# Output phase of an attention kernel: the product with the reciprocals moves ahead of the moments on DVE, and the packing of denominators moves ahead of two other transfers on the sync engine

## The reference

```python
q = q * dh ** (-0.5)
sim1 = jnp.einsum('bhid,bhjd->bhij', q, k_l)
attn1 = jax.nn.softmax(sim1, axis=-1)
out = attn1 @ attn2_inv @ (attn3 @ v)
res = conv_general_dilated(v, conv_w, ...)      # 33 taps along the tokens, one filter a head
out = (out + res).transpose(0, 2, 1, 3).reshape(b, n, h * dh)
out = out @ w_out + b_out
return x + out
...
t = t + _L1_attn_ref(_ln_t(t), ...)             # then t + _L1_ffn_ref(_ln_t(t), ...)
```

## Time and profile before

| | |
|---|---|
| median of 3 runs | 6015.71 us (6015.61 to 6017.85) |
| the profiled execution | 6021.51 us, span 6019.8 us |
| busy in the span | PE 5283.7 us, ACT 3257.7 us, DVE 2981.2 us, POOL 1675.8 us |
| DVE's first and last `o_t` of the output phase | 2643.2 us and 3699.1 us |
| DMA | 755.65 MB in all, a mean of 126 GB/s |

### The profile page before, as it was taken

The page is one execution under the profiler, slowest core; times in us unless marked ns, Lnnn a source line. Parts: engine busy times, 40 slices in busy tenths (PEclk is TensorE's granted clock), DMA queues, the critical chain, the costliest instruction groups (busy, mean ns, idle before and its releaser), DMA issues. The chain is left out here.

```text
span 6019.8 us, 209173 instructions
## 1 busy us (share of the span) xinstructions
PE 5283.7 (88%) x90148; PEld 3236.3 (54%) x90240; DVE 2981.2 (50%) x7660; ACT 3257.7 (54%) x9351; POOL 1675.8 (28%) x2016
## 2 busy tenths in 40 slices
PE   5499999997788887789999997888888888888888
PEld 4499888896566665654444443333333333333333
DVE  8577777775778775568888885000000000000000
ACT  5355555564677775369999995333333333333333
POOL 2000000002877874348777784000000000000000
PEclk7799999999999999999999998999999999999999
DMA  8622111225777773358887874111111111111111
GB/s 362 273 101 81 57 57 57 78 83 183 239 238 239 228 237 104 96 142 229 228 229 228 228 220 120 41 48 47 48 47 45 48 47 48 47 45 50 45 48 31
DMA packets 857847, 755.65 MB, mean 126 GB/s; under 512 B 71024, under 2 KB 732528, under 8 KB 853872
## 3 DMA queue, kind: packets, MB, share of 16 engines
q1 hardware_dynamic: 841840, 642.91, 35.9%
q0 software_dynamic: 13664, 99.32, 4.1%
q10 hardware_dynamic: 1440, 0.33, 0.0%
HBM read 425.72 MB, written 308.45 MB: 122 GB/s over the span
## 5 line engine op out<-in xcount | busy, mean ns | idle before, releaser
L2607 ACT ACTIVATE f_y<-f_acc 128x16 f32<-128x16 f32 x4096 | 753.7, 184 | 1545.3 <-PE f_acc L2573 1545.3
L2573 PEld LDWEIGHTS f_acc<-f_y,f_vT 128*32 128x32 f32 x32768 | 645.0, 108 | 1491.0 <-ACT f_y L2607 1491.0
L2573 PE MATMUL f_acc<-f_y,f_vT 128*32 128x16 f32 x32768 | 1045.9, 193 | 296.6 <-ACT f_y L2607 0.4
L2562 PE MATMUL f_junk<-f_idle 128*32 128x512 bf16 x12368 | 1225.5, 376 | 1.1 <-issue 1.1
L2518 DVE TENSOR_TENSOR f_sum<-f_turned,f_t 128x512 f32<-128x512 f32 x128 | 88.5, 692 | 2071.2 <-PE f_turned L2555 2071.1
L2272 DVE TENSOR_REDUCE o_m<-o_bank_l 128x8 bf16<-128x512 f32 x512 | 327.4, 680 | 101.2 <-PE o_bank_l L2038 101.1
L2562 PEld LDWEIGHTS f_junk<-f_idle 128*32 128x32 bf16 x12368 | 368.1, 99 | 1.4 <-issue 1.4
L1184 ACT ACTIVATE a_p<-a_s 128x512 f32<-128x512 f32 x512 | 264.1, 602 | 180.7 <-PE a_s L1068 180.7
L470 POOL DMA_DIRECT2D hidden<-l_h x46 | 34.6, 754 | 1166.9 <-DVE l_hsum L730 961.5
L653 ACT ACTIVATE l_gate<-l_pf,l_bf 128x256 f32<-128x256 f32 (+7 forms) x512 | 202.4, 446 | 229.6 <-PE l_pf L580 229.4
L2223 ACT ACTIVATE o_p<-o_bank_s 128x512 f32<-128x512 f32 x512 | 264.4, 602 | 34.0 <-PE o_bank_s L2061 33.0
(11 more groups left out here) (284 smaller groups left out, 11562.0 us busy)
## 6 DMA issues: line engine op xcount, KB each, us to landing
o_v<-vals SPq DMA_DIRECT2D x256, 272.0 KB, 3.5
a_hid<-hidden SPq DMA_DIRECT2D x112, 520.0 KB, 5.1
skew<-gn_skew POOLq DMA_DIRECT2D x8, 6144.0 KB, 23.3
hidden<-l_h POOLq DMA_DIRECT2D x46, 1040.0 KB, 6.7
l_x<-skew SPq DMA_DIRECT2D x46, 1024.0 KB, 5.3
vals<-a_v SPq DMA_DIRECT2D x128, 272.0 KB, 3.3
gn_x<-in_x SPq DMA_DIRECT2D x16, 2048.0 KB, 17.0
a_xin<-in_x SPq DMA_DIRECT2D x128, 256.0 KB, 5.0
```

Source lines behind the costliest of these rows:

```text
L2562: nc.tensor.matmul(junk[rows, :], idle[:, 0:QUAD], idle[:, :], start=True, stop=True)
L2573: mm = nc.tensor.matmul(acc[k % 2][rows, t, :], vT[:, rows], before, start=False, stop=True, skip_group_check=True)
L2607: nc.scalar.activation(y[q][:, u, :], acc[u // RC % 2][:, u % RC, :], ACT.Sigmoid).then_inc(s_y, 1)
```

## The change

Two orders are changed, and no instruction is added or removed. On DVE, `residual` is cut in two: the aggregation into mean and variance becomes `moments`, and `normalise` is called between the two. On SP, `pack` is called right behind `spread`, ahead of `load_v` and `broadcast`.

```diff
@@ SP, slot
                 if precedes(c, 1, first):
                     spread(b, c - 1)
-
+                pack(b, c)
                 if c < GT and b + 1 < B:
                     wait(sp, "conv", NG * (b + 1))
                     load_v(b + 1, 1, c)
@@
                     load_v(b + 2, 0, c - GT)
                 if precedes(c, 1, first):
                     broadcast(b, c - 1)
-                pack(b, c)
@@ DVE, residual
                 for k in range(GT):
                     nc.vector.bn_stats(st[:, k, :], out[:, k, :])
+
+            def moments():
                 dve.drain()
                 for k in range(GT):
                     ms = nc.vector.bn_aggr(mv[:, k, :], st[:, k:k + 1, :])
@@ DVE, slot
                 if precedes(c, 3, first):
                     residual(b, c - 3)
+                if precedes(c, 2, first):
+                    normalise(b, c - 2)
+                if precedes(c, 3, first):
+                    moments()
                 if precedes(c, 1, first):
                     reciprocals(b, c - 1)
                 if precedes(c, 2, first):
-                    normalise(b, c - 2)
                     add_convolved(b, c - 2)
```

## The result

The changed kernel takes 6261.99 us in the median of 4 runs (6253.48 to 6264.83), the kernel before 6015.66 us in runs beside it. The ratio is 1.0406, with a 95% interval of 1.0394 to 1.0419: 4% slower. The prediction was 6150 us, with a range to 6212 us. The direction was right, and so was the ring on DVE; the size was not. The profiled execution has a span of 6263.0 us, 243.2 us more than before.

The account below looks back on a forecast made before the run. PE was taken as the bound, its floor 8.27 us of an 8.38 us slot; the change closes a DVE ring of 9.50 us. 114 slots x 1.12 = 128, plus 6 in the last image: 6015.7 + 134 = 6150 us, range 6080 to 6212.

Parts of the forecast that it names:

- the ring on DVE: Output phase: reciprocals wait behind a product whose broadcast needs the previous reciprocals; 9.50 us a slot against 8.38; 80%.
- the landing: Time from the broadcast's issue until its data is in `o_rden`, taken as 4.6 us within 3.5 to 5.6.
- The collision with `o_z`: DVE's product slowed by POOL's `o_z`, 1.30 instead of 0.63 us; the change was to save 0.67 in such slots.
- the wait for denominators: DVE's reciprocals waiting for packed denominators, 12.4 us in 24 of 107 slots; SP's earlier packing was to remove it.
- the forecast of 9.50: Output-phase slot in us, once around DVE's ring: 1.32 + 0.03 + 3.52 + 4.6 + 0.03, against 8.38 before.
- The 20 waits at L1876: SP's waits before the stores, ended by the previous broadcast's landing; read as putting that landing at 5.2 us.
- The heavier rival: Broadcast behind `o_v` always lands in 5.6 us, giving a 10.5 us slot and 6263 us; 6%.
- "landing shortens as the load thins out" rival: Less busy DMA engines land the broadcast in 3.5 to 3.9 us; slot 8.40 to 8.80, 6018 to 6070 us; 10%.
- SP's order: Packing ahead of `o_v` loads and broadcast: packing not waiting for ACT, broadcast issued 0.4 us later.
- The o_v loads: Later loads could hold up PE's convolution twice an image; costed at nothing, without PE's idle cover at most 30 us.
- The port pair: Skill rule: two-SBUF-input DVE and GpSimd operations lock each other out; by that alone the change could only gain.
- the price of a transfer: Skill's 2.0 us plus bytes by 436 GB/s, 2.6 us for 256 KB; ring 7.5 us, PE staying the bound.

Follow-up runs that it names:

- changed_two_recips: Changed kernel with two HBM buffers for `recips` and a semaphore each, so the stores wait for the broadcast before the last: 6259.8 us, ratio 1.0406.
- dve_alone: Changed kernel with SP's old order, so only DVE's order is new: 6094.3 us, ratio 1.012.
- pack_between_v_and_bcast: Changed kernel with SP's packing moved between the `o_v` loads and the broadcast: 6184.6 us, ratio 1.0276.
- tokens_moved: Changed kernel with the `o_xnT` load moved from behind the broadcast to ahead of the stores to `recips`: 6215.4 us, ratio 1.0329.
- v_quarter: Changed kernel with a quarter of the rows in each `o_v` load of the loop over groups; the output differs: 6144.8 us, ratio 1.0208.
- dve_old_v_first: Kernel before, keeping DVE's old order, with SP issuing `o_v`, stores, packing, broadcast: 6134.7 us, ratio 1.0191.
- sp_alone_two_recips: Kernel before with only SP's new order, plus two HBM buffers for `recips` with a semaphore each: 6062.8 us, ratio 1.0073.
- bcast_before_v: Changed kernel with SP's broadcast ahead of the `o_v` loads (stores, packing, broadcast, `o_v`): 6230.2 us, ratio 1.0354.

## Why the prediction was wrong in size

**The ring.** Right. Six kernels have the product ahead of the reciprocals and no other wait that matters. In each, the slot is the sum around the ring: 1.42 us from the product's start to the reciprocals' end, the way from there to the broadcast's issue, the landing, and 0.10 from the landing to the product (all means over the events and issues of the trace).

| kernel | slot, us | reciprocals to issue | landing | sum |
|---|---|---|---|---|
| changed | 10.44 | 3.64 | 5.29 | 10.45 |
| changed_two_recips | 10.43 | 3.63 | 5.29 | 10.44 |
| dve_alone | 9.01 | 2.77 | 4.73 | 9.02 |
| pack_between_v_and_bcast | 9.67 | 3.82 | 4.34 | 9.68 |
| tokens_moved | 10.03 | 3.63 | 4.87 | 10.02 |
| v_quarter | 9.42 | 3.56 | 4.34 | 9.42 |

The collision with `o_z` and the wait for denominators went, as predicted. They had cost DVE 20.6 and 12.4 us in 900, and this shows nowhere in a slot that the ring sets.

**The landing: the term that failed.** The prediction had "Landing of the broadcast: I take 4.6, the middle between 3.5 and 5.6 or slightly above it." It measured 5.29. Of the 0.94 us that a slot exceeds the forecast of 9.50, this is 0.69. The term was read off a trace in which the broadcast had about 0.9 us of pause behind `o_v` and two tiny DMAs behind it. The change took both away. I allowed for the first only ("slightly above") and had not thought of the second. The trace of the kernel before bears this out: its 13 broadcasts that were issued within 0.3 us behind `o_v`, with the packing behind them, landed in 4.65 us in the mean. So 4.6 was about right for the lost pause alone. The runs show 0.95 us for a smaller `o_v` (v_quarter) or an earlier one (pack_between_v_and_bcast) and 0.4 for one transfer less behind (tokens_moved). Each was measured by itself, and they need not add up. Without the neighbour ahead the landing is back at the old one, without one of those behind less than half of the way back. The rest of the 0.94 is small: 0.10 in DVE's part (1.42 for 1.32), 0.09 in the issues (3.64 for 3.55) and 0.07 from the landing to the product (0.10 for 0.03).

One reading behind the term was wrong as well. The 20 waits at L1876 were taken for slots in which the way from reciprocals to landing filled the whole slot, which gave 5.2 us. But SP comes to that wait from the issue of `o_base`, before the reciprocals have ended: in 19 of the 20 the landing came first, and its mean there is 4.8 us.

**The heavier rival**, 6263 us at 6%, hit the time, by luck in its reasons: its landing of 5.6 us was too long and its other terms too small. Its one row had a pause of 0.68 us behind `o_v` and the packing behind it, as is usual in that kernel; so it wasn't a sample of the new condition, and no run shows what made it long.

**The "landing shortens as the load thins out" rival** is refuted. The DMA engines' share fell from 0.80 to 0.65 and the landing rose: what counts is what stands in the queue around the broadcast, not the mean load. The row of the DMA view for `o_xnT` rose too, from 3.5 to 5.1 us.

**SP's order.** "The broadcast goes out 0.4 us later than before" was nearly right (3.64 for 3.15 us in the mean), and the packing did not wait for ACT. But I costed SP's order only as a term of DVE's ring. Alone it costs 88 us, through a ring of its own that I had a row for (L1876) and read only as a bound on the landing. The halves alone cost 75 and 88 us, the whole 246 us: each half lengthens what the other has made critical.

**The o_v loads** cost nothing, as said: PE waited 11 us for them in 900 and had the room.

**The port pair and the price of a transfer.** The Trainium skill's rule on the shared port pair ("SBUF — State Buffer", "SBUF: two separate sides") agrees with the traces here: a product that starts alone takes 0.63 to 0.69 us, and one that starts while `o_z` runs takes up to 1.57 us, and nearly always ends 0.55 to 0.70 us behind the end of `o_z`. By that alone the change would have gained; it did not decide. The Trainium skill's price ("DMA: Bandwidth & Descriptors", "Anatomy of one DMA"), an estimate of 2.6 us for 256 KB from its figures for DMAs that GpSimd issues, is half of what the broadcast measured in the queue, 5.3 us; the measurement decides.

## What to carry to other kernels

Before an instruction that waits for a DMA is moved ahead of another one, ask whether the DMA depends on the other one of the slot before. If so, the move closes a ring, and the slot becomes the sum around it; draw each ring through every in-order queue, the sync engine's too, and sum it. Read a DMA's landing for the neighbours it will have, not those it had: a 256 KB transfer took 4.3 us behind small loads and 5.3 us with 544 KB directly ahead and another 256 KB directly behind, at a lower mean load.

## What the runs showed of the hardware

- What is issued behind a DMA can delay it too: with one 256 KB transfer less in the 2 us behind it, the broadcast landed 0.4 us earlier (tokens_moved).
- In dve_old_v_first, as the last of six large transfers in a row, the two `o_v` issues took 1.69 us in the mean, against 1.07 in the kernel before. They took 1.34 in dve_alone, without such a row, so the cause is open.
- A DVE product with two inputs in SBUF that starts while POOL's `o_z` (1.04 us) runs ends 0.55 to 0.70 us behind it, and so takes 0.69 to 1.56 us, by how much of `o_z` is left (64 products of sp_alone_two_recips).
- In the two kernels in which PE stood still for up to 5.8 us at the halves of `v`, the granted clock between 2700 and 3600 us had a mean of 0.93. Around the pause that ended at 3014.73 in bcast_before_v it was 0.50, which is the lower of PE's two levels (1.2 and not 2.4 GHz), and the eight matmuls behind the pause took 1.98 us instead of 1.13. In the changed kernel the mean was 0.99, in dve_alone and pack_between_v_and_bcast 1.00.
